# Normed feed-forward: the scale parameter moves from a GpSimd multiplication into VectorE's subtraction of the mean, and rstd moves into VectorE's shift

## The reference

```python
h = silu(bitlinear158(x, w1, b1))          # 256 -> 1024
h = gelu(h)                                # exact form
mu = mean(h); var = mean((h - mu)**2)
h = (h - mu) * rsqrt(var + 1e-5) * ln_g + ln_b
out = bitlinear158(h, w2, b2)              # 1024 -> 256
# bitlinear158: RMS norm of the row, round to 8 bits by the row's largest value, times ternary weights
```

## Time and profile before

| quantity | value |
|---|---|
| median of three runs | 2513.76 us |
| the profiled execution's own time | 2522.49 us |
| its span, first to last instruction | 2520.6 us |
| VectorE busy | 1622.3 us (64%) |
| TensorE busy | 1518.6 us (60%) |
| ScalarE busy | 1062.1 us (42%) |
| GpSimd busy | 613.7 us (24%) |
| mean granted TensorE clock | 0.792 of full |

### The profile page before, as it was taken

One profiled execution on the slowest core, in us unless ns is written; L12 is line 12 of the kernel. 1 busy time (PEld: TensorE's weight loads), 2 busy tenths in 40 slices (PEclk: granted clock), 3 DMA queues, 4 the chain that ended last, 5 costly groups with the idle time before them and its releaser, 6 DMA issues. The chain is left out here.

```text
span 2520.6 us, 34997 instructions
## 1 busy us (share of the span) xinstructions
PE 1518.6 (60%) x11260; PEld 924.7 (37%) x11260; DVE 1622.3 (64%) x3141; ACT 1062.1 (42%) x1453; POOL 613.7 (24%) x862
## 2 busy tenths in 40 slices
PE   1069999994995787874334343279999367620022
PEld 1035555552774544542112112135555233310011
DVE  6457777773453477675777887445555487856787
ACT  4427667673221334344355455323333377710022
POOL 4312233332002223223333433201010011105500
PEclk9999999996998788897555556689999688855555
DMA  6635555542001221211000000001100100003001
GB/s 179 173 77 117 119 120 119 119 114 76 1 0 30 51 60 40 47 43 56 10 1 1 0 0 0 21 29 31 29 25 23 51 1 0 1 21 61 6 26 41
DMA packets 94652, 120.97 MB, mean 48 GB/s; under 512 B 25868, under 2 KB 78284, under 8 KB 89932
## 3 DMA queue, kind: packets, MB, share of 16 engines
q1 hardware_dynamic: 94540, 119.56, 19.0%
HBM read 79.75 MB, written 22.09 MB: 40 GB/s over the span
## 5 line engine op out<-in xcount | busy, mean ns | idle before, releaser
L571 DVE TENSOR_REDUCE ratt_nmax<-ratt_psS 128x2 f32<-128x512 f32 x512 | 319.9, 684 | 112.6 <-PE ratt_psS L463 112.0
L537 ACT ACTIVATE ratt_E<-ratt_psT 128x1024 f32<-128x1024 f32 x256 | 255.6, 1022 | 123.9 <-PE ratt_psT L485 123.8
L463 PE MATMUL ratt_psS<-ratt_K,ratt_Q 72*128 72x256 bf16 x1024 | 210.7, 291 | 54.4 <-DMA ratt_K<-ratt_ones 48.5
L485 PE MATMUL ratt_psT<-ratt_Q,ratt_K 75*128 75x256 bf16 x1024 | 202.6, 283 | 15.2 <-DMA ratt_Q<-ratt_rows 14.8
L498 PE MATMUL ratt_psO<-ratt_E,ratt_V 128*32 128x256 f32 x2048 | 144.8, 403 | 0.7 <-ACT ratt_E L537 0.7
L463 PEld LDWEIGHTS ratt_psS<-ratt_K,ratt_Q 72*128 72x128 bf16 x1024 | 82.3, 101 | 154.2 <-issue 94.0
L1833 PE MATMUL nffn_psH<-nffn_W,nffn_QT 128*128 128x512 bf16 x128 | 57.7, 601 | 114.6 <-DVE nffn_H L1797 95.8
L485 PEld LDWEIGHTS ratt_psT<-ratt_Q,ratt_K 75*128 75x128 bf16 x1024 | 102.4, 101 | 36.2 <-issue 16.8
L1316 PE MATMUL gatt_psA<-gatt_DA,gatt_same 128*128 128x512 f32 x128 | 89.1, 786 | 25.3 <-DVE gatt_DB L1201 25.3
L1135 POOL TENSOR_TENSOR gatt_DA<-gatt_own,gatt_a 128x1024 f32<-128x1024 f32 x32 | 61.5, 1935 | 143.4 <-PE gatt_psA L1319 90.4
L1756 POOL TENSOR_TENSOR nffn_H<-nffn_H,nffn_gam 128x1024 f32<-128x1024 f32 x32 | 93.1, 2937 | 7.4 <-DVE nffn_H L1788 7.4
(11 more groups left out here) (451 smaller groups left out, 4124.3 us busy)
## 6 DMA issues: line engine op xcount, KB each, us to landing
ratt_Q<-z_parts SPq DMA_DIRECT2D x32, 576.0 KB
ratt_K<-context_parts SPq DMA_DIRECT2D x96, 192.0 KB
gatt_V<-in_ctx_dram SPq DMA_DIRECT2D x16, 512.0 KB, 6.9
z_parts<-prep_ZS SPq DMA_DIRECT2D x48, 128.0 KB, 2.7
context_parts<-prep_CS SPq DMA_DIRECT2D x48, 128.0 KB
head_sums<-ratt_O SPq DMA_DIRECT2D x64, 72.0 KB
all_X<-in_x_dram SPq DMA_DIRECT2D x8, 512.0 KB, 4.8
prep_C<-in_ctx_dram SPq DMA_DIRECT2D x8, 512.0 KB, 5.6
```

The lines of the kernel that those rows point to most:

```text
L463: mm = nc.tensor.matmul(psS[:, RING[h], c * D:(c + 1) * D], Q9[0:R, buf, h, k % 2, c * P:(c + 1) * P], K9[0:R, buf, h, k % 2, :], start=Tr ...
L485: mm = nc.tensor.matmul(psT[:, p % 2, e, c, :], K9[0:RM, buf, h, u, c * P:(c + 1) * P], Q9[0:RM, buf, h, u, :], start=True, stop=True)
L537: nc.scalar.activation(E[:, 2 * b + p // 2, 2 * (p % 2):2 * (p % 2) + 2], psT[:, p % 2], ACT.Exp, scale=SCALE).then_inc(exped, 1)
L571: nc.vector.tensor_reduce(nmax[:, k % 2, h, :], psS[:, RING[h]].rearrange("p (c t) -> p c t", c=2), AX.X, ALU.max, negate=True).then_inc(m ...
```

## The change

Three edits, all in `normed_ffn`:

1. L1788's `tensor_scalar` (H - mean) * rstd becomes a `scalar_tensor_tensor` (H - mean) * gam. It no longer waits for rstd.
2. GpSimd's four multiplications by gam (L1756) and the semaphore that they waited on go.
3. L1801's `tensor_tensor` H + bet becomes a `scalar_tensor_tensor` H * rstd + bet. The first one of a group waits for rstd.

```diff
-                        for j in range(G):
-                            pool.wait_ge(normed, b * G + j + 1)
-                            nc.gpsimd.tensor_tensor(H[:, bw, j], H[:, bw, j], gam[:], ALU.mult).then_inc(gained, 1)
                         down.power(pool, b)
...
-                        dve.wait_ge(rstd_done, b + 1)
                         dve.wait_ge(agg, b * G + G)
                         for j in range(G):
-                            v.tensor_scalar(H[:, bw, j], H[:, bw, j], mv[:, j, 0:1], rstd[:, j:j + 1],
-                                            ALU.subtract, ALU.mult).then_inc(normed, 1)
+                            v.scalar_tensor_tensor(H[:, bw, j], H[:, bw, j], mv[:, j, 0:1], gam[:],
+                                                   ALU.subtract, ALU.mult).then_inc(gained, 1)
...
                             dve.wait_ge(gained, b * G + j + 1)
-                            v.tensor_tensor(H[:, bw, j], H[:, bw, j], bet[:], ALU.add).then_inc(shifted, 1)
+                            if j == 0:
+                                dve.wait_ge(rstd_done, b + 1)
+                            v.scalar_tensor_tensor(H[:, bw, j], H[:, bw, j], rstd[:, j:j + 1], bet[:],
+                                                   ALU.mult, ALU.add).then_inc(shifted, 1)
```

More of the change, by code:

```diff
@@ L1735, in normed_ffn @@
         psH = s.ps("psH", [P, 2, HALF])
-        (uw_done, up, affined, silued, gelued, agg, veps_done, rstd_done, normed, gained, shifted, b2_added) = (
+        (uw_done, up, affined, silued, gelued, agg, veps_done, rstd_done, gained, shifted, b2_added) = (
             s.sem(x) for x in ("uw_done", "up", "affined", "silued", "gelued", "agg2", "veps2_done",
-                               "rstd2_done", "normed2", "gained", "shifted", "b2_added"))
+                               "rstd2_done", "gained", "shifted", "b2_added"))
         with nc.Block() as block:
```

## The result

The changed kernel takes 2478.88 us (median of four runs, 2471.14 to 2484.01); the kernel before, with one more run, 2515.25. The ratio is 0.9853 with a 95% interval of 0.9817 to 0.9888, so between 1.1% and 1.8% faster. The forecast was 2476. The profiled execution took 2484.01 us (span 2482.2), to be held against 2522.49 (span 2520.6).

What follows compares the result with a forecast made beforehand. VectorE was taken to bound the normed feed-forward. Saving 4.43 us a step over seven steps (31.0) plus 6.6 in the last gave 37.6 us, so 2476 us from a median of 2513.76; range 2467 to 2489.

Steps and rivals of the forecast that it cites:

- The wait ahead of the subtractions: VectorE's idle time for rstd between the aggregations and L1788, 1.41 us, was to go, leaving 0.10 us.
- The stretch of L1788 by GpSimd: GpSimd's multiplications by gam were said to stretch L1788's four instructions (mean 1818 ns; 695 ns for a similar one elsewhere).
- Rival 4: L1788 wasn't stretched by GpSimd and its replacements also take 1.82 us: 22 us lost of 37.6, 2498; chance 0.03.
- The count by rates alone (2520): L1788's replacement costs 17 us more by instruction rates, less 11.3 us of waits: about 6 us slower, 2520.
- The four new instructions: L1788's replacements at 1.22 us each, 1.14 us start to start: 4.56 us to the first affine half, against 6.95.
- Rival 2: Two SBUF inputs at 1024 columns run at half the rate, 2.29 us an instruction: slower, 2545; chance 0.02.
- The first shift and the others: L1801: the first shrinks from 2.05 to 1.22 us; the changed operation itself costs nothing, 1.22 for 1.22 us.
- rstd in time: GpSimd's rstd ready before the first shift, some 3 us ahead, or just in time if all four instructions pass first.
- Rival 1: rstd's small GpSimd work and VectorE's two-input work obstruct each other in full: 8 x 1.2 = 9.6 us, 2486; chance 0.14.
- Who is late next: ScalarE's 10.07 us idle ahead of its first Silu loses 4.4; everything behind the first L1646 keeps its distances.
- rival 3: Part of ScalarE's or TensorE's step isn't held by VectorE's first half; half the gain is lost: 2495; chance 0.04.
- The clock: TensorE's granted clock varies between steps, 1.7 us a step; half of seven steps allowed, 6 us either way.

## Why the prediction was right

- *The wait ahead of the subtractions.* Put at 0.10 us in place of 1.41: it is 0.03. Putting it back brought the 1.41 again.
- *The stretch of L1788 by GpSimd*: shown by leaving the multiplication out (1818 to 808 ns), and, on the new instructions, by putting GpSimd's work back (4.90 to 9.07 us). Rival 4, that L1788 was slow by itself, is out. The prediction read too much into the mean, though: "never got that rate here" is wrong. The first two of the four took 0.81 us each, the second of them already under way when GpSimd began at 1343.16, and only the last two took 2.8:

```profile
1342.27 0.81 DVE L1788 TENSOR_SCALAR nffn_H<-nffn_H,nffn_mv,nffn_rstd 128x1024 f32<-128x1024 f32 x1 [1.41 <-POOL nffn_rstd L1753]
1343.00 0.81 DVE L1788 TENSOR_SCALAR nffn_H<-nffn_H,nffn_mv,nffn_rstd 128x1024 f32<-128x1024 f32 x1
```

The count by rates alone (2520) failed because it took all four at that rate, and not because the rate was never reached.
- *The four new instructions*: 4.56 us to the first affine half forecast, 4.83 measured (1377.39 to 1382.22). The line through 256 and 1024 columns joined unlike rows: the one with 256 has a per-partition operand (`qffn_yunit`), the one with 1024 has none, and that operand costs 50 ns in each of eight instructions a step. Like with like it is 480 and 1272 ns, a little over a nanosecond a column. Rival 2, half the rate, is out: 1.27 us and not 2.29.
- *The first shift and the others*: forecast at 1.22, measured 1.27; this is the other half of the same miss. In all, a step's middle shrank by 4.10 us where 4.43 was forecast, and the last step by 6.31 where 6.6 was. 35.0 us instead of 37.6.
- *rstd in time*: no idle time at the first shift. GpSimd's addition was not late (0.20 us), its power was (1.87), though both began inside VectorE's first instruction; the forecast had both late. The longest of VectorE's four took 1.32 us against 1.27. Rival 1 is out: the engines' turns cost VectorE hundredths of a microsecond here, where I had charged 0.10 and the rival 1.2.
- *Who is late next*: I said that everything behind keeps its distance. That failed in one place: in five steps ScalarE's Gelus end 0.4 to 0.6 us after VectorE is ready for them. It cost 3 us. This is as much as came true of rival 3 (half the gain lost): nothing waited inside the middles.
- *The clock*: 6 us allowed either way. Over this block's tails it gave 2.3 us net, less than the 3 us of waits for Gelu; outside it, blocks with unchanged code gave 4.2 us of span, and that the clock did it isn't shown. The forecast of the whole was nearer than its parts, and that is luck: the 2.6 us that the middles fell short were made up by what nobody had forecast (2.3 - 3.0 + 4.2).
- *GpSimd's busy time*: 520 us forecast, 527.1 measured; the difference is the eight powers that got longer.

## What to carry to other kernels

Two engines whose instructions take turns are one resource: 11.6 us of GpSimd's elementwise work cost VectorE 4.9 us a step (middle 24.05, against 19.16 with the work left out), and doing it inside VectorE's own instructions, with the same wait, costs 2.1 (21.30). Moving it to VectorE as instructions of its own gained nothing (ratio 0.9999), so it is the fusion that pays, and that needed the scalar operands to be shared out anew between two instructions. A mean over a group can hide two kinds of instructions, here 0.81 and 2.83 us behind one 1818 ns: read them one by one before concluding. And a wait can cost more than its length where TensorE runs in bursts (18.2 us of block for 10.8 us of waiting here): price it by the path, then allow for the granted clock of what comes behind.

## What the runs showed of the hardware

- A VectorE instruction with two inputs in SBUF is stretched by a GpSimd instruction on unrelated data as much as a `tensor_scalar` is (1.27 to 2.33 us mean of all, 0.81 to 1.82; to 3.35 and 2.83 where they meet, since they take turns by whole instructions), one with an input in PSUM (1.40 for two halves) or with one input and a tiny output (1.22) not at all. The Trainium skill, "GPSIMD Engine Reference", section "Key points", names both kinds, the instruction with two SBUF inputs and the one in a two-port mode, as those that contend with GpSimd; the traces agree as far as both instructions were stretched, and that the `tensor_scalar` ran in a two-port mode isn't seen in them.
- A per-partition operand costs a `scalar_tensor_tensor` about 50 ns (median 1218 against 1272). A `tensor_scalar` with two such operands took 808 ns where one with none, in another block, takes 695; no run changes only that.
- Identical code twice gave a block equal to 0.01 us (371.31 and 371.31), with the clock rising in the same steps. Which steps get a rise depends on the program's timing in a way that these runs do not explain: without idle matmuls, with a middle of 19.95 us most tails had it, with 21.3 us only the seventh, with 24.9 us none, with 23.7 and 24.05 us some.
- 19 idle matmuls of 128x512 a step, placed where TensorE is free ahead of its chain of transposes and products, were worth 13 to 15 us to the changed kernel, the difference of its medians (2478.9 and 2481.3) to 2466.2, and 8 us to the kernel before (2516.0 in the same series to 2508.3).
